# A decoder layer for 128 sequences: the feed-forward of the last two groups turned by TensorE instead of by DMA, the x2 bias a step of its own, and all steps in a new order

## What is computed

```python
q, k, v = x @ Wq + bq, x @ Wk + bk, x @ Wv + bv          # 16 heads of 64
q_, k_  = exp(q @ wq_feat), exp(k @ wk_feat)             # 32 features a head
x1  = LN(x  + ((q_ @ (k_.T @ v)) / (q_ @ k_.sum() + 1e-6)) @ Wproj + bproj)
x2  = LN(x1 + softmax(Q K.T / sqrt(8)) V @ Wo + bo)      # Q from x1, K and V from ctx, 16 heads of 8
h   = gelu(x2 @ ternary(W_fc).T)                         # 128 -> 512, weights -1, 0, 1
out = LN(x2 + layernorm(h, ln_w, ln_b) @ ternary(W_proj).T)
```

## Time and profile before

| | us |
|---|---|
| three runs, median (lowest, highest) | 743.17 (742.66, 746.18) |
| the profiled execution, its own time | 746.38 |
| its span, first to last instruction | 742.9 |
| PE busy in the span | 685.4 |
| DVE, ACT, POOL busy | 527.6, 447.2, 408.5 |

### The profile page before, as it was taken

The page is one execution under the profiler, slowest core; times in us unless marked ns, Lnnn a source line. Parts: engine busy times, 40 slices in busy tenths (PEclk is TensorE's granted clock), DMA queues, the critical chain, the costliest instruction groups (busy, mean ns, idle before and its releaser), DMA issues.

```text
span 742.9 us, 31000 instructions
## 1 busy us (share of the span) xinstructions
PE 685.4 (92%) x13506; PEld 487.3 (66%) x13506; DVE 527.6 (71%) x1476; ACT 447.2 (60%) x782; POOL 408.5 (55%) x442
## 2 busy tenths in 40 slices
...
GB/s 302 17 45 31 18 31 17 65 50 79 45 31 103 17 116 19 73 54 79 48 31 101 19 107 25 75 45 87 45 25 110 17 75 30 39 53 44 74 56 85
DMA packets 97161, 44.29 MB, mean 60 GB/s; under 512 B 87810, under 2 KB 87939, under 8 KB 96899
## 3 DMA queue, kind: packets, MB, share of 16 engines
...
## 4 chain that ended last, share of the span: by engine, by line
PE 72%; POOL 10%; DVE 5%; issue 5%; DMA 5%; ACT 1%; SPq 0%; POOLq 0%; DVEq 0%; ACTq 0%
PE bank L302 12%; PE bank L319 7%; PE bank L292 6%; PE bank L361 4%; DMA x2T<-x2s 4%; POOL gall L931 3%; PE bank L403 3%; PE bank L346 2%; PE bank L388 2%; POOL gs L936 2%; PE bank L315 2%; PE bank L427 2%; PE bank L434 2%; PE bank L435 2%; PE bank L339 2%
## 5 line engine op out<-in xcount | busy, mean ns | idle before, releaser
L931 POOL TENSOR_TENSOR gall<-gall,lnr 128x512 f32<-128x512 f32 x64 | 80.7, 1283 | 85.5 <-DVE st L756 85.5
L302 PE MATMUL bank<-Mh,GT 128*32 128x128 f32 x4096 | 124.4, 273 | 0.3 <-DVE GT L737 0.3
L302 PEld LDWEIGHTS bank<-Mh,GT 128*32 128x32 f32 x4096 | 110.3, 110 | 16.7 <-issue 15.3
L900 POOL TENSOR_SCALAR ve<-mv 128x4 f32<-128x4 f32 x64 | 12.4, 194 | 160.3 <-DVE mv L763 157.5
L786 DVE TENSOR_REDUCE mx<-bank 128x8 f32<-128x512 f32 x128 | 78.1, 681 | 12.6 <-PE bank L361 12.6
L737 DVE COPY GT<-bank 128x512 f32<-128x512 f32 x81 | 52.4, 682 | 36.7 <-PE bank L292 26.4
L936 POOL TENSOR_TENSOR gs<-gall,gs 128x512 f16<-128x512 f32 x64 | 73.4, 1160 | 8.4 <-ACT gs L607 8.1
L580 ACT ACTIVATE PT<-bank 128x512 f32<-128x512 f32 x128 | 64.5, 627 | 8.9 <-PE bank L388 8.9
L903 POOL TENSOR_TENSOR rstd<-ve,mhalf 128x4 f32<-128x4 f32 x64 | 66.9, 1045 | 5.3
L319 PE MATMUL bank<-Cb,qT 128*64 128x128 f32 x1024 | 66.8, 273 | 0.0
L292 PE MATMUL bank<-kp,xs 64*128 64x512 f32 x256 | 63.8, 616 | 0.0
...
## 6 DMA issues: line engine op xcount, KB each, us to landing
...
gT<-gs SPq DMA_TRANSPOSE x64, 2.8
...
```

The source lines that it names most:

```text
L302: m = e.matmul(bk[32 * j:32 * j + 32, tile(g_)], GT[b % 4][:, tile(hh, 32)], Mh[:, tile(hh)], start=True, stop=True)
L931: e.tensor_tensor(g[t][:, :], g[t][:, :], lnr[:, :], ALU.mult).then_inc(s_gs, 1)
```

## The change

Four things. (1) In groups 14 and 15 alone (`by_pe`), x2 is turned by four PE transposes (`flip3`): ACT copies the upper f16 half out of PSUM, DVE subtracts to get the rest, both straight into `x2T`. (2) In the same two groups `g` is turned by PE, `turn0` to `turn3`, four transposes each: step c takes column block c of all four tiles, ACT writes the scaled upper half, DVE the scaled rest, into `gT`. `gs`, `gh`, `gl`, POOL's split of x2 and five DMA transposes are gone for each of the two groups. All four `turn` stand before the first `down`. (3) The x2 bias, which followed POOL's split inside `ap2`, is a step `ab2`. (4) `HEAD`, `PERIOD` and `TAIL` are ordered anew; in the other 14 groups the same instructions are issued as before.

```diff
 HEAD = """
-small1 wb wk bias2 wq k0@0 k1@0 WkT zeros split@0 k2@0 mh0 g0+@0 g1@0 g2@0 g3@0 mh1 bv q0@0 nbeta q1@0 gam k3@0 small2 c0+@0 c1+@0 ks+@0 c2@0 q2@0
-kst@0 loadx@0 q3@0 WqT g4@0 g5@0 g6@0 g7@0 Wvp c3@0 Wff c4+@0 loadx@1 split@1 c5+@0 dT@0 c6+@0 xb@0 c7+@0 biasA loadc@0 bc0@0 loadx@2 bc1@0 bc2@0 bc3@0
-bias3 sbar
+small1 wb wk wq WkT k0@0 zeros nbeta k1@0 k2@0 k3@0 g0+@0 loadx@0 WqT g1@0 g2+@0 g3+@0 bv mh0 mh1 q0@0 gam q1@0 split@0 ks+@0 c0+@0 q2@0 kst@0 q3@0
+bias2 g4+@0 Wvp g5+@0 g6+@0 g7+@0 dT@0 c1@0 split@1 loadx@1 c2@0 c3@0 loadc@0 small2 c4+@0 c5+@0 c6@0 c7+@0 biasA bc0@0 bc1@0 Wff bc2@0 loadx@2 bc3@0
+sbar bias3 xb@0
 """
 PERIOD = """
-k0 k1 down0@4 k2 k3 down1@4 down2@4 score0@2 loadc score1@2 o0@1 o1@1 o2@1 o3@1 rows@2 split@-1 q0 st1@1 q1 down3@4 q2 g0+ ap2@3 g1+ xb g2+ g3 prob0@2
-gs0@3 prob1@2 ks gs1@3 ap1@1 c0+ q3 st3@4 up0@3 up1@3 kst up2@3 gl0@3 up3@3 flip@1 loadx@-2 gh0@3 gl1@3 stat@3 c1+ pv0@2 c2+ dT ap3@4 pv1@2 g4 gh1@3 g5
-g6 g7 qproj@1 kproj@1 ab1@1 gs2@3 oturn0@2 c3 c4+ c5+ c6 gh2@3 c7+ oturn1@2 gs3@3 bc0 bc1 bc2 gl2@3 gl3@3 bc3 cturn0+@2 gh3@3 cturn1+@2 vproj@1 proj0@2
-proj1@2 st2@2
+k0 k1 k2 down0@4 down1@4 score0@2 score1@2 o0@1 o1@1 split@-1 o2@1 xb o3@1 rows@2 ap2@3 q0 k3 ab2@3 down2@4 st1@1 down3@4 q1 g0 g1+ g2 g3+ prob0@2
+ap1@1 prob1@2 ks st3@4 c0+ ap3@4 q2 up0@3 gs0@3 flip@1 up1@3 up2@3 up3@3 stat@3 q3 gs1@3 kst pv0@2 gl0@3 c1+ c2+ pv1@2 c3 gs2@3 dT gl1@3 loadc g4+
+gh0@3 g5+ g6 g7 qproj@1 gl2@3 oturn0@2 kproj@1 gh1@3 oturn1@2 c4+ gs3@3 c5 c6 gh2@3 c7 bc0 bc1 bc2 bc3 cturn0+@2 cturn1+@2 gl3@3 ab1@1 vproj@1 loadx@-2
+proj0@2 proj1@2 st2@2 gh3@3
 """
...
-down0@4 dT@1 c3+@1 gl3@4 ap3@5 g4+@1 g5@1 g6+@1 g7+@1 bc0@1 bc1@1 st2@3 bc2@1 bc3@1 rows@2 c4+@1 c5+@1 c6+@1 ap2@3 c7+@1 down1@4 down2@4 down3@4
-prob0@2 st3@4 prob1@2 o0@1 o1@1 o2@1 o3@1 up0@3 st1@1 up1@3 up2@3 up3@3 gs0@3 pv0+@2 pv1+@2 gs1@3 gl0@3 gl1@3 gs2@3 stat@3 oturn0@2 gh0@3 ap1@1
-oturn1@2 gh1@3 cturn0+@2 flip+@1 cturn1@2 proj0@2 proj1@2 st2@2 qproj@1 gh2@3 gl2@3 down0@3 down1@3 gs3@3 ap2@2 score0@1 gh3@3 vproj@1 score1@1 down2@3
-gl3@3 ab1@1 rows@1 ap3@4 up0@2 gs0@2 gs1@2 up1@2 up2@2 up3@2 gs2@2 down3@3 prob0@1 prob1@1 gs3@2 gh0@2 pv0+@1 gl0@2 gl1@2 stat@2 gh1@2 pv1@1 oturn0@1
-gl2@2 oturn1@1 cturn0+@1 cturn1+@1 proj0@1 proj1@1 st2@1 gl3@2 down0@2 gh2@2 ap2@1 st3@3 down1@2 gs0@1 gs1@1 gh3@2 down2@2 ap3@3 gl0@1 gl1@1 down3@2
-up0@1 gs2@1 up1@1 up2@1 gh0@1 gs3@1 up3@1 st3@2 gl2@1 gh1@1 gl3@1 stat@1 ap3@2 gh2@1 down0@1 down1@1 down2@1 down3@1 st3@1 gh3@1 ap3@1
...
+c6+@1 c7+@1 prob0@2 gs1@3 prob1@2 o0@1 o1@1 o2@1 o3@1 up0@3 st1@1 up1@3 up2@3 up3@3 pv0+@2 gl0@3 pv1+@2 stat@3 oturn0@2 gh0@3 oturn1@2 kproj@1 gs2@3
+ap1@1 cturn0@2 cturn1@2 flip@1 gh1@3 proj0@2 proj1@2 st2@2 gl1@3 qproj@1 gh2@3 gl2@3 ap2@2 score0@1 gh3@3 gs3@3 score1@1 flip3@2 ab2@2 down0@3 vproj@1
+gl3@3 down1@3 ab1@1 rows@1 up0@2 up1@2 up2@2 down2@3 up3@2 down3@3 prob0@1 prob1@1 pv0+@1 st3@3 stat@2 pv1+@1 oturn0@1 oturn1@1 ap3@3 cturn0+@1
+cturn1+@1 proj0@1 proj1@1 st2@1 turn0@2 ab2@1 turn1@2 turn2@2 ap2@1 turn3@2 flip3@1 down0@2 down1@2 down2@2 down3@2 up0@1 st3@2 up1@1 stat@1 up2@1
+up3@1 turn0@1 turn1@1 turn2@1 turn3@1 ap3@2 down0@1 down1@1 down2@1 down3@1 st3@1 ap3@1
...
+            def flip3(s):
+                bk, done = start("flip3", s)
+                for t in range(4):
+                    w.wait_ge(s_ln["2"], 4 * s + t + 1)
+                    m = e.transpose(bk[:, tile(t)], x2[s % 2][:, tile(t)], ident[:, :])
+                m.then_inc(done, 1)
...
+            def turn(s, c):
+                bk, done = start("turn", s, c)
+                for t in range(4):
+                    w.wait_ge(*emptied("up", s, t))
+                    m = e.transpose(bk[:, tile(t)], g[t][:, tile(c)], ident[:, :])
+                m.then_inc(done, 1)
...
+            def turn(s, c):
+                if s > 0:
+                    w.wait_ge(*filled("down", s - 1, 3))
+                w.wait_ge(*filled("turn", s, c))
+                b3 = bank[uses["turn", s, c][0]][:, :].rearrange("p (t n) -> p t n", t=4)
+                e.activation(gTc[c][:, :, 0, :], b3, ACT.Copy, scale=lnw[:, c:c + 1]).then_inc(s_ghp, 1)
...
+            def turn(s, c):
+                w.wait_ge(s_ghp, 4 * by_pe.index(s) + c + 1)
+                b3 = bank[uses["turn", s, c][0]][:, :].rearrange("p (t n) -> p t n", t=4)
+                e.scalar_tensor_tensor(gTc[c][:, :, 1, :], b3, lnw[:, c:c + 1], gTc[c][:, :, 0, :], ALU.mult, ALU.subtract).then_inc(emptied("turn", s, c)[0], 1)
...
-                w.wait_ge(s_x2l, s + 1)
+
+            def ab2(s):
+                if s in by_pe:
+                    w.wait_ge(*filled("flip3", s))
+                    w.wait_ge(s_ln["2"], 4 * s + 4)
+                else:
+                    w.wait_ge(s_x2l, s + 1)
                 w.wait_ge(*emptied("bias3", 0))
-                addbias(x, x, bias3).then_inc(s_x2b, 1)
+                addbias(x2[s % 2], x2[s % 2], bias3).then_inc(s_x2b, 1)
```

More of the change, by code:

```diff
@@ L28 @@
 WIDE = {"score": 4, "prob": 4, "mh": 2}
-BANKED = "k q ks kst dT bc g c o flip kproj vproj qproj score rows prob pv oturn cturn proj up down wq wk wb mh biasA bias2 nbeta gam bias3 sbar".split()
-WHOLE = "small1 small2 ab1 st1 st2 st3 ap1 ap2 ap3 bias2 bias3".split()
+BANKED = "k q ks kst dT bc g c o flip kproj vproj qproj score rows prob pv oturn cturn proj flip3 up turn down wq wk wb mh biasA bias2 nbeta gam bias3 sbar".split()
+WHOLE = "small1 small2 flip3 ab1 ab2 st1 st2 st3 ap1 ap2 ap3 bias2 bias3".split()
@@ L51 @@
-gl3@3 ab1@1 rows@1 ap3@4 up0@2 gs0@2 gs1@2 up1@2 up2@2 up3@2 gs2@2 down3@3 prob0@1 prob1@1 gs3@2 gh0@2 pv0+@1 gl0@2 gl1@2 stat@2 gh1@2 pv1@1 oturn0@1
-gl2@2 oturn1@1 cturn0+@1 cturn1+@1 proj0@1 proj1@1 st2@1 gl3@2 down0@2 gh2@2 ap2@1 st3@3 down1@2 gs0@1 gs1@1 gh3@2 down2@2 ap3@3 gl0@1 gl1@1 down3@2
-up0@1 gs2@1 up1@1 up2@1 gh0@1 gs3@1 up3@1 st3@2 gl2@1 gh1@1 gl3@1 stat@1 ap3@2 gh2@1 down0@1 down1@1 down2@1 down3@1 st3@1 gh3@1 ap3@1
+k0@1 k1@1 score0@3 ap2@4 score1@3 kproj@2 o0@2 o1@2 o2@2 ab2@4 o3@2 rows@3 g0@1 st1@2 gs0@4 gs1@4 g1@1 down0@5 down1@5 up0@4 up1@4 down2@5 up2@4 up3@4
@@ new lines @@
+down3@5 gl0@4 ap1@2 prob0@3 prob1@3 stat@4 gl1@4 c0+@1 c1@1 pv0@3 g2+@1 g3@1 st3@5 k2@1 gh0@4 flip+@2 loadc@1 q0@1 gs2@4 oturn0@3 gh1@4 k3@1 qproj@2
+q1@1 c2+@1 c3@1 pv1+@3 ks+@1 gh2@4 score0@2 score1@2 q2@1 vproj@2 gs3@4 gl2@4 xb@1 gl3@4 g4+@1 g5+@1 down0@4 q3@1 kst@1 gh3@4 oturn1@3 g6@1 ab1@2 ap3@5
+g7@1 cturn0+@3 cturn1+@3 dT@1 down1@4 proj0@3 proj1@3 st2@3 down2@4 down3@4 bc0@1 bc1@1 bc2@1 bc3@1 rows@2 c4+@1 st3@4 c5+@1 ap2@3 ap3@4 ab2@3 gs0@3
+c6+@1 c7+@1 prob0@2 gs1@3 prob1@2 o0@1 o1@1 o2@1 o3@1 up0@3 st1@1 up1@3 up2@3 up3@3 pv0+@2 gl0@3 pv1+@2 stat@3 oturn0@2 gh0@3 oturn1@2 kproj@1 gs2@3
@@ L465, in pe_program @@
                     sbar()
-                elif name in ("ks", "kst", "dT", "flip", "kproj", "qproj", "vproj", "rows"):
-                    {"ks": ksum, "kst": ksum_turn, "dT": denom, "flip": flip, "kproj": kproj, "qproj": qproj, "vproj": vproj, "rows": rows}[name](s)
+                elif name in ("ks", "kst", "dT", "flip", "kproj", "qproj", "vproj", "rows", "flip3"):
+                    {"ks": ksum, "kst": ksum_turn, "dT": denom, "flip": flip, "kproj": kproj, "qproj": qproj, "vproj": vproj, "rows": rows, "flip3": flip3}[name](s)
                 elif name in BANKED:
                     {"k": kexp, "q": qexp, "bc": broadcast, "g": gmat, "c": cmat, "o": outp, "score": score, "prob": prob, "pv": pv,
-                     "oturn": oturn, "cturn": cturn, "proj": proj, "up": up, "down": down}[name](s, t)
+                     "oturn": oturn, "cturn": cturn, "proj": proj, "up": up, "turn": turn, "down": down}[name](s, t)
         def act_program(e):
@@ L621, in act_program @@
                     nbeta_()
[L622 to L625 removed]
+                elif name in ("kproj", "qproj", "vproj", "rows", "flip3"):
+                    {"kproj": kproj, "qproj": qproj, "vproj": vproj, "rows": rows, "flip3": flip3}[name](s)
+                elif name in ("k", "q", "prob", "up", "gh", "turn"):
+                    {"k": kexp, "q": qexp, "prob": prob, "up": up, "gh": ghi, "turn": turn}[name](s, t)
                 elif on_act and name in ("ks", "flip"):
@@ L853, in dve_program @@
                 elif name in ("bc", "o", "score", "oturn", "proj", "turn", "down"):
-                    {"bc": broadcast, "o": outp, "score": score, "oturn": oturn, "proj": proj, "down": down}[name](s, t)
+                    {"bc": broadcast, "o": outp, "score": score, "oturn": oturn, "proj": proj, "turn": turn, "down": down}[name](s, t)
         def pool_program(e):
```

50 lines of the change are left out of this document (34 added, 16 removed).

## The result

| | before | after |
|---|---|---|
| median of four runs (lowest, highest), us | 742.92 (742.66, 746.18) | 722.62 (721.58, 722.94) |
| profiled execution: its own time, its span | 746.38, 742.9 | 722.81, 720.8 |
| PE busy | 685.4 | 685.5 |
| POOL busy | 408.5 | 385.5 |

The ratio is 0.9717, with an interval of 0.9694 to 0.974: 20.3 us less by the medians, 22.1 by the two spans. (Times won with an interval go by the ratio, not by the two medians, so they differ a little from these: 0.9717 is 21.0 us.) PE did the same work, so everything won is idle PE.

A forecast was written before the change was run, and what follows sets the result against it. PE, busy 92% of the span, was taken to bound the body, loads the head, one dependent chain the tail. 11.1 + 3.1 + 2.5 + 1.0 = 17.7 us off gave 725.5 us against the median, range 718 to 736.

The forecast's parts named there:

- the tail: After 660 us, one dependent chain through all engines: 11.1 us won after the last proj and 3.1 before it.
- The head: Start of the kernel, waiting for loads: earlier weights let k0 start near 12.1; 2.5 us won, between 0 and 4.5.
- the body: PE-bound steady periods: 3 us won from x2T waits, 2 lost to new waits; 1 us, between 9 lost and 4 won.
- rival D: Fast side: clock up early in the head, no wait in the body; 719 us, chance 0.13 (716 to 722).
- The end: From group 15's last proj matmul to the finish: 25.95 us instead of 37.05, 11.1 us won.
- The pieces of `turn`: DVE and ACT operations turning g in the last two groups: 0.75 us each on DVE, 0.7 on ACT, 1.0 allowed.
- rival C: Turning does not shorten the end: pieces of 1.5 us or low clock, 5 won, 731.5 us; 0.22 jointly with another rival.
- The stretch to the last `proj`: From 660 to 705.85 us: kproj@1 moved, qproj and maxima earlier; 3.1 us won, between 1 and 4.5.
- three thin places: Steps in one period with half a microsecond or less to spare: kst 0.6, c4 0, bc2 0.45 us.
- No 17.5 us row: Sign of being right: PE's waits from 600 to 743 hold no 17.5 us for gT, only a few of 1 to 3.
- `rows` DMAs 41.7 us apart: Sign of being right, in the steady periods: the distance between the DMAs of rows is 41.7 us.
- signs of a wrong prediction: PE waiting at dT, cturn or up some ten times; turn pieces over 1 us; rows DMAs over 42.3 us apart.

The follow-up runs named there:

- e5_turn_only: The kernel after, but x2 of groups 14 and 15 split by POOL and turned by DMA again, only g by PE: 724.29 us, ratio 0.9755.
- e1_head: The kernel before with the new HEAD alone, PERIOD and TAIL as before: 741.40 us, ratio 0.9977.
- e2_period: The kernel before with the new PERIOD alone, HEAD and TAIL as before: 739.60 us, ratio 0.9947.
- e7_ap2_early: The kernel before with x2's normalising and splitting moved right behind rows and split in PERIOD: 740.26 us, ratio 0.9967.
- e3_tail: The kernel before with the new TAIL alone, last two groups turned by PE, HEAD and PERIOD as before: 730.94 us, ratio 0.9827.

## Why the prediction was right, and where its terms were off

The forecast was 725.5 us, the measurement 722.62, near the fast edge of the forecast band (722 to 729); in spans 17.7 us less was forecast and 22.1 came. That the tail brings most held. The head and the body changed places, though: by the runs of one string the tail won 12.8 (14.2 forecast), the body 3.9 (1.0) and the head 1.7 (2.5), so the sum is better than its terms, and part of that is luck. No rival's time came true; of rival D, the fast side, the two conditions did (full clock early in the head, no wait in the body), without all that it had priced for them.

- **The end: 11.1 forecast, 10.2 measured.** When the new trace is shifted by 11.93 us (705.85 - 693.92), the steps follow the forecast within 0.3 us up to `flip3@1`: `ap2@1` ends at 710.63 (forecast 710.9), `flip3@1` at 712.38 (712.35). Then two steps were off and cancelled, which is luck. `down@2`'s matmuls start 0.107 us apart, at 1.2 GHz, and end 1.4 us late, where the prediction had taken 2.4 GHz. The table load, which the prediction put on the path with 1.28 us, ran right behind ACT's copy for `flip3`, while PE was still at `down@2`: ACT's Gelu end at 717.46 (717.3). The last part lost 0.9: the fourth `turn` piece ends at 722.2 (721.7), since `stat@1` stands ahead of the four pieces on DVE until 707.50 although ACT has the first one ready at 706.6; and `down@1` ran at the low clock, for which the prediction had taken a value between. As to `flip3` itself, the 5.9 us that the prediction had on the way through POOL and the DMA were hidden beside `down@2` but for 0.4 (`e5_turn_only`).
- **The pieces of `turn`: 0.75 taken, 0.66 to 0.74 measured** on DVE and 0.60 on ACT (0.7 taken), so rival C with 1.5 us had no ground; its bound of 1.0 was wide. The 16 transposes of a group took 1.91 us, some 0.11 us each. The Trainium skill (TensorE: Matmul & The Clock Gate, Part 4: PE-mode transpose) gives about 390 ns for one in bf16 in isolation. The prediction's estimate from it, 6.2 us for 16, took that figure for the distance between transposes in a row, which it is not here; the 3.5 us that it would have cost did not appear.
- **`ap2@1`: 1.11 forecast with POOL idle, 1.10 measured.** The same four pieces of group 14 took 3.71 with POOL on `gs` (the row is below, with what was new).
- **The stretch to the last `proj`: 3.1 forecast**, of which the 0.9 of `kproj@1` lie ahead of the mark `o0@1`; so 2.2 was forecast from there on, and 2.8 came. Shifted by the 9.16 us of that mark, `qproj@1` ends at 676.3 (forecast 678.9, before 680.4) and the eight maxima at 688.5 (forecast 689.2, before 691.6). The first step won more than was counted, 4.1 us for 1.5, and `ap2@2`, which stands between the two on DVE, took 3.71 us in place of 1.76 and gave part of it back. PE waits 3.8 us once for DVE's part of `qproj@1` (2.5 in the kernel before) and 1.3 at `flip3@2` for the maxima (2.1 before, at `rows`). No run separates these parts.
- **The head: 2.5 forecast, 1.5 in the trace, 1.7 (0.5 to 3.0) by `e1_head`.** `k0` started at 12.43 (12.1 forecast), as the profile of PE's head shows:
```profile
5.55 7.09 PE L186 MATMUL bank<-small,Qm 128*128 128x64 f32 x32 [2.17 <-DMA Qm<-in_WkT]
12.43 0.63 PE L246 MATMUL bank<-Wkfh,xh 128*128 128x512 f16 x1
12.86 0.63 PE L247 MATMUL bank<-Wkfl,xh 128*128 128x512 f16 x1
...
13.71 3.38 PE L225 MATMUL bank<-Qm,PT 128*128 128x128 f32 x16
16.93 0.38 PE L246 MATMUL bank<-Wkfh,xh 128*128 128x512 f16 x1
17.14 0.38 PE L247 MATMUL bank<-Wkfl,xh 128*128 128x512 f16 x1
```
Both folds run without a pause, as forecast, but the first began 0.9 us later than in the earlier trace rows, since WkT landed later; and `nbeta`'s 16 matmuls, now at the front, start some 0.2 us apart. Full speed was there at `k1`, as hoped.
- **The body: 1.0 forecast, the largest error.** 3.9 us (2.5 to 5.5) by `e2_period`. The 3 us for x2T were right (`e7_ap2_early`: 2.5). The failed step is the other one, "I take 3 us won and 2 lost": none of the three thin places, `kst`, `c4`, `bc2`, is in the list of PE's waits of the kernel after between 60 and 600. The count of one period had given 0.6, 0 and 0.45 us of room, and the margin of half a microsecond was charged as if it were a wait. In the two traces the middle differs by 7.6 us, but 0.9 of it is `kproj@1`, and the profiled execution of before was itself 3.5 above its median of 742.92. Its 8.1 us of "issue" stops are the most of all traces: with the same `PERIOD` they were 5.7 and 6.6 in `e3_tail` and `e1_head`, and with the new one 5.8 to 7.3. So the step from 8.1 to 5.9 can't be put down to the change.
- **What was to show it.** No 17.5 us row: right. 26 us from the last `proj` to the end: 26.9. `rows` DMAs 41.7 us apart: 41.2, and 41.7 stands in kernels with the old `PERIOD` too, so this sign could not tell. `k0` at 12: 12.4. None of the signs of a wrong prediction appeared.
